# Edge stage of a graph convolution: second layer on the two halves of the array, first layer for four pairs at once

## What is computed

```python
h = silu(edge_scalars @ fc_w1 * (1.0 / sqrt(8))) * 1.679      # 8 -> 64
w = h @ fc_w2 * (1.0 / sqrt(64))                              # 64 -> 256
w_a, w_b, w_c, w_d = w[:, :64], w[:, 64:128], w[:, 128:192], w[:, 192:]
mid0 = w_a * xg0 * ea0
mid1 = w_b * einsum('euc,ec->eu', xg1, ea1) * INV_SQRT3
mid2 = (w_c * xg0)[:, :, None] * ea1[:, None, :]
mid3 = (w_d * ea0)[:, :, None] * xg1
agg = segment_sum(concat(mid0, mid1, mid2, mid3), edge_dst)   # 512 wide
```

## Time and profile before

| | |
|---|---|
| median of the runs | 4875.23 us |
| profiled execution, its time | 4926.35 us |
| its span | 4924.5 us |
| PE busy | 3152.5 us, 64% |
| DVE busy | 3139.1 us, 64% |
| POOL busy | 2963.7 us, 60% |
| ACT busy | 2579.5 us, 52% |
| mean granted clock of PE | 0.794 |
| instructions | 58380 |

### The profile page before, as it was taken

The page is one execution under the profiler, slowest core; times in us unless marked ns, Lnnn a source line. Parts: engine busy times, 40 slices in busy tenths (PEclk is TensorE's granted clock), DMA queues, the critical chain, the costliest instruction groups (busy, mean ns, idle before and its releaser), DMA issues. The chain is left out here.

```text
span 4924.5 us, 58380 instructions
## 1 busy us (share of the span) xinstructions
PE 3152.5 (64%) x11125; PEld 1913.5 (39%) x11125; DVE 3139.1 (64%) x8102; ACT 2579.5 (52%) x7839; POOL 2963.7 (60%) x3014
## 2 busy tenths in 40 slices
PE   4699989999999874545555565555354555555550
PEld 3344444444444563333433343333233333333340
DVE  7788888888888755454555554568354554555558
ACT  3588889888888522333333343345233343334347
POOL 2356656556556303667676676747667777776656
PEclk8899999999999987677767676678667777777675
DMA  5223233223223224444444444424444444444435
GB/s 165 90 83 86 84 86 88 84 85 87 83 84 90 75 82 125 121 118 129 122 122 127 116 126 128 116 72 138 117 115 128 128 116 129 127 115 128 120 91 160
DMA packets 274559, 540.42 MB, mean 110 GB/s; under 512 B 73156, under 2 KB 161983, under 8 KB 274240
## 3 DMA queue, kind: packets, MB, share of 16 engines
q0 software_dynamic: 134912, 376.36, 28.1%
q1 hardware_dynamic: 132308, 154.29, 10.0%
q10 hardware_dynamic: 7020, 6.40, 0.4%
HBM read 495.47 MB, written 41.31 MB: 109 GB/s over the span
## 5 line engine op out<-in xcount | busy, mean ns | idle before, releaser
L1174 POOL DMA_INDIRECT arena<-h_rows,idx x1856 | 1891.1, 1019 | 1070.9 <-issue 510.4
L1309 PE MATMUL ps<-arena,z 128*128 128x264 f32 x3712 | 1338.2, 514 | 455.3 <-DVE arena L1421 305.1
L768 POOL DMA_INDIRECT arena<-y_rows,idx x928 | 890.7, 960 | 730.1 <-ACT arena L799 361.5
L1233 ACT ACTIVATE z<-z 128x256 f32<-128x256 f32 x928 | 382.3, 412 | 1548.1 <-PE ps L1309 547.9
L1309 PEld LDWEIGHTS ps<-arena,z 128*128 128x128 f32 x3712 | 864.1, 251 | 694.1 <-DVE arena L1421 364.4
L1429 DVE TENSOR_TENSOR z<-ps,z 128x264 f32 x928 | 396.7, 427 | 1136.0 <-remote 378.7
L797 ACT ACTIVATE arena<-arena 128x128 f32<-128x128 f32 x2784 | 914.9, 399 | 12.7 <-issue 7.8
L842 PE MATMUL ps<-arena 128*128 128x512 f32 x1856 | 895.6, 606 | 14.5 <-issue 9.0
L1225 ACT ACTIVATE z<-iota,dst_x 128x128 f32<-128x128 f32 x1856 | 644.1, 394 | 26.4
L1421 DVE TENSOR_TENSOR arena<-arena,z 128x520 f32<-128x520 f32 x928 | 639.9, 690 | 2.1 <-ACT z L1214 1.3
L842 PEld LDWEIGHTS ps<-arena 128*128 128x128 f32 x1856 | 361.1, 196 | 485.4 <-issue 473.1
(11 more groups left out here) (229 smaller groups left out, 3070.1 us busy)
## 6 DMA issues: line engine op xcount, KB each, us to landing
z<-lo_rows SPq DMA_DIRECT2D x116, 512.0 KB
arena<-h_rows,idx POOLq DMA_INDIRECT x1856
arena<-y_rows,idx POOLq DMA_INDIRECT x928
z<-seg_rows SPq DMA_DIRECT2D x232, 64.0 KB
h_rows<-arena SPq DMA_DIRECT2D x98, 132.0 KB, 1.7
arena<-h_rows SPq DMA_DIRECT2D x98, 132.0 KB, 2.5
res_rows<-z SPq DMA_DIRECT2D x98, 128.0 KB, 1.9
arena<-res_rows SPq DMA_DIRECT2D x98, 128.0 KB, 2.1
```

The costliest lines, as they stand in the source:

```text
L768: pool.indirect_dma_start(out=ring[:, r, :], out_offset=None, in_=s.y_rows, in_offset=bass.IndirectOffsetOnAxis(ap=rows_of[:, u, n:n + 1], ...
L1174: pool.indirect_dma_start(out=ring[:, u * SCORED + n, :], out_offset=None, in_=h_rows, in_offset=bass.IndirectOffsetOnAxis(ap=s.idx[:, u, ...
L1233: nc.scalar.activation(sel[:, q % SELS, :, :].rearrange("p k n -> p (k n)"), away[:, q % 2, :, :].rearrange("p k n -> p (k n)"), ACT.Relu, ...
L1309: last = t.matmul(ps[:, bank[q % 4], 0:ROW], sel[:, q % SELS, k, :], ring[:, u * SCORED + 2 * q + k, :], start=(k == 0), stop=(k == 1))
```

## The change

In `conv_edges` alone:

- `second` is issued per quad: for each of its two pairs two matmuls, one on rows 0 to 63 and one on rows 64 to 127 of `h2` and `w2`, 256 columns each. `w2` is now fc_w2 twice, one under the other (128 x 256), without the zero blocks and their memset. The two slots of a pair go to two neighbouring banks (1 and 2, or 3 and 4 by quad), both pairs of a quad side by side in each. w_ok counts quads.
- `first` does four pairs (an octet) in one bank, 512 columns; with only one bank for it, it waits for the SiLU of the octet before. pre_ok and h_ok count octets.
- `silu` is one activation of 512 columns per octet, two `h2` buffers, the second in room freed by `w2` and next to it.
- PE's order: at pairs p with p % 4 = 3 `first` for octet (p + 9) // 4; at odd p `second` for the quad of pairs p + 3 and p + 4; then `collect`. ACT's order: the SiLU of octet p/4 + 1 ahead of `scaled`(p) for p % 4 = 0.
- `collect`, its three banks, and all of DVE's instructions but one memset stay; DVE's wait for w_ok counts quads, SP's for pre_ok octets.

```diff
-    h2 = s.arena[:, 8960:9472].rearrange("p (q a e) -> p q a e", q=2, a=2)
     tail = s.arena[:, 9472 + 4 * SLOT_COLS:2 * SCORED * ROW]
     ring = tail[:, 0:RING * FEAT].rearrange("p (r f) -> p r f", f=FEAT)
...
     ps = s.ps
-    w2 = tail[:, RING * FEAT + 4 * P:RING * FEAT + 8 * P]
-    pre = lambda quad: ps[:, quad % 2, 0:256]
-    layer2 = lambda pair: ps[:, 2 + pair % 3, :].rearrange("p (k f) -> p k f", k=2)
+    w2 = tail[:, RING * FEAT + 4 * P:RING * FEAT + 6 * P]
+    h2 = [s.arena[:, 8960:9472], tail[:, RING * FEAT + 6 * P:RING * FEAT + 10 * P]]
+    hidden = lambda pair: h2[pair // 4 % 2][:, pair % 4 * P:(pair % 4 + 1) * P]
+    pre = ps[:, 0, :]
+    halves = lambda quad: ps[:, 1 + quad % 2 * 2:3 + quad % 2 * 2, :]
+    layer2 = lambda pair: halves(pair // 2)[:, :, pair % 2 * FEAT:(pair % 2 + 1) * FEAT]
     collected = lambda pair: ps[:, 5 + pair % 3, :]
 
     with nc.Block() as block:
...
             for n in range(GROUP):
                 sp.dma_start(w8[8 * n:8 * n + 8, n // 2, n % 2 * 64:n % 2 * 64 + 64], a["fc_w1"]).then_inc(wt, 16)
...
+                sp.dma_start(w2[h * 64:(h + 1) * 64, :], a["fc_w2"]).then_inc(wt, 16)
             for pair in range(PAIRED):
 
...
-                    sp.wait_ge(pre_ok, (g - 1) * 4)
+                    sp.wait_ge(pre_ok, (g - 1) * 2)
                     sp.wait_ge(got8[u], g // 2 * 128)
...
-            def silu(quad):
-                act.wait_ge(pre_ok, quad + 1)
-                if quad >= 2:
-                    act.wait_ge(w_ok, 2 * (quad - 1))
-                nc.scalar.activation(h2[:, quad % 2, :, :].rearrange("p a e -> p (a e)"), pre(quad), ACT.Silu,
-                                     scale=1.0 / math.sqrt(8.0)).then_inc(h_ok, 1)
+            def silu(octet):
+                act.wait_ge(pre_ok, octet + 1)
+                if octet >= 2:
+                    act.wait_ge(w_ok, 2 * (octet - 1))
+                nc.scalar.activation(h2[octet % 2], pre, ACT.Silu, scale=1.0 / math.sqrt(8.0)).then_inc(h_ok, 1)
 
...
             silu(0)
-            silu(1)
             for pair in range(PAIRED):
-                quad = (pair - 3) // 2 + 2
-                if pair >= 3 and pair % 2 and quad < QUADS:
-                    silu(quad)
+                if pair % 4 == 0 and pair // 4 + 1 < OCTETS:
+                    silu(pair // 4 + 1)
                 if pair % 8 == 1 and pair // 8 + 3 < GROUPS:
                     stage(pair // 8 + 3)
                 scaled(pair)
...
-            def first(quad):
-                g, q = quad // 4, quad % 4
-                u = g % 2
-                if q == 0:
+            def first(octet):
+                g, u = octet // 2, octet // 2 % 2
+                if octet % 2 == 0:
                     pe.wait_ge(got8[u], (g // 2 + 1) * 128)
+                if octet >= 1:
+                    pe.wait_ge(h_ok, octet)
+                for n in range(4):
+                    last = nc.tensor.matmul(pre[:, n * P:(n + 1) * P], w8[:, octet % 2 * 4 + n, :], e8[:, u, :], start=True, stop=True)
+                last.then_inc(pre_ok, 1)
+
+            def second(quad):
+
+                pe.wait_ge(h_ok, quad // 2 + 1)
                 if quad >= 2:
-                    pe.wait_ge(h_ok, quad - 1)
-                for b in range(2):
-                    last = nc.tensor.matmul(pre(quad)[:, b * P:(b + 1) * P], w8[:, 2 * q + b, :], e8[:, u, :], start=True, stop=True)
-                last.then_inc(pre_ok, 1)
-
-            def second(pair):
-                quad = pair // 2
-                pe.wait_ge(h_ok, quad + 1)
-                if pair >= 3:
-                    pe.wait_ge(msg_ok, pair - 2)
-                nc.tensor.matmul(ps[:, 2 + pair % 3, :], h2[:, quad % 2, pair % 2, :], w2, start=True, stop=True).then_inc(w_ok, 1)
+                    pe.wait_ge(msg_ok, 2 * quad - 2)
+                for pair in (2 * quad, 2 * quad + 1):
+                    for k in range(2):
+                        rows = slice(k * 64, (k + 1) * 64)
+                        last = nc.tensor.matmul(layer2(pair)[:, k, :], hidden(pair)[rows, :], w2[rows, :], start=True, stop=True)
+                last.then_inc(w_ok, 1)
 
             def collect(pair):
                 pe.wait_ge(msg_ok, pair + 1)
@@ -842,24 +845,22 @@
                     last = nc.tensor.matmul(collected(pair), sel[:, pair % 4, k, :], msg[:, pair % 4, k, :], start=(k == 0), stop=(k == 1))
                 last.then_inc(agg_ok, 1)
 
-            for quad in range(4):
-                first(quad)
-                if quad < 2:
-                    second(2 * quad)
-                    if quad < 1:
-                        second(1)
+            first(0)
+            for quad in range(2):
+                second(quad)
+            first(1)
+            first(2)
             for pair in range(PAIRED):
-                if pair % 2 == 0 and pair // 2 + 4 < QUADS:
-                    first(pair // 2 + 4)
-                if pair + 3 < PAIRED:
-                    second(pair + 3)
+                if pair % 4 == 3 and (pair + 9) // 4 < OCTETS:
+                    first((pair + 9) // 4)
+                if pair % 2 and (pair + 3) // 2 < QUADS:
+                    second((pair + 3) // 2)
                 collect(pair)
 
...
             v.memset(s.w8[:, :], 0.0).then_inc(wz, 1)
-            v.memset(w2, 0.0).then_inc(wz, 1)
             v.memset(s.z[:, 0:BLOCKS * 512], 0.0).then_inc(zero_ok, 1)
...
                 v.tensor_tensor(vt, x[:, :, 448:512], x[:, :, 512:576], ALU.add).then_inc(v_ok, 1)
-                dve.wait_ge(w_ok, pair + 1)
+                dve.wait_ge(w_ok, pair // 2 + 1)
                 if pair >= 4:
                     dve.wait_ge(agg_ok, pair - 3)
                 three = lambda t: t.rearrange("p k (c f) -> p k c f", c=3)
```

4 lines of the change are left out of this document (2 added, 2 removed).

## The result

| | before | changed |
|---|---|---|
| median of the runs | 4876.36 us (4 runs) | 4950.77 us (4939.11 to 4959.67, 4 runs) |
| ratio | | 1.0126, 95% interval 1.0100 to 1.0153 |
| profiled execution | 4926.35 us | 4959.67 us |
| mean granted clock | 0.794 | 0.791 |

The forecast was 4774, in a range of 4690 to 4900: wrong in sign and outside the range. One sentence for everything that follows: the chips on which these kernels were measured differ, the kernel before taking 4459 to 4463 us on three and 4876 to 4918 on the others (these runs among them), so times are compared within one series only.

What follows compares the result with a forecast made beforehand. The prediction took PE, at 2.795 of 3.178 us a pair, to bound the edge stage. A lower floor (-30 us) and absorbed lateness (-71) gave -101, set against the median 4875.23: 4774 us, range 4690 to 4900.

Steps and rivals of the forecast that it cites:

- What bounds the kernel: Edge stage: PE is slowest at 2.795 us a pair of 3.178; the other 0.383 is stalls, 178 us over the stage.
- `second`: PE's second-layer matmuls: 0.86 us a pair becomes 0.54 by partial overlap of the halves, plus 0.16 for row switches.
- PE's sum: PE's time in the edge stage after the change: 2.64 us a pair, between 2.37 and 2.96 by the bounds.
- The floor: Slowest engine of the edge stage after the change: DVE with 2.73 us a pair instead of PE, ACT right behind.
- The gain of the floor: Edge stage: moving the bound from PE to DVE saves 0.065 us a pair over 464 pairs, 30 us.
- Lateness: Edge-stage stalls from late PE signals, taken as given: more slack absorbs four tenths of 178 us, a gain of 71 us.
- The bound that I had set aside: Edge-stage stalls: none of the 178 us is gained if lateness grows with the slack, as where PE's queue sets it.
- the size of the slack: Lateness consumers can bear: DVE 1.3 us before, 5 after, for its weights from PE.
- The SiLU's slack: ACT's room for late PE signals before its SiLU's wait for w_ok: 3.8 us before, 7.7 after.
- Rival 3: PE's `second`: halves don't overlap and switches are paid, 0.165 us a pair more, +77 us, 4952; chance 0.14.
- Rival 2: Edge stage: lateness follows PE's instruction count, 16 to 20 a pair, stalls 178 to 222 us, +14, 4889; chance 0.10.

Runs made afterwards that it cites:

- halves_apart: Changed kernel with the 64-row matmuls reordered, all of rows 0 to 63 first, then rows 64 to 127: 4428.28 us, ratio 0.9932 to the kernel before.
- second series: Runs on one chip with PE's signals on time: the unaltered changed kernel took 4429.71 us against 4458.93 for the kernel before, ratio 0.9933.
- octets_only: Kernel before with only `first` and SiLU per four pairs in one bank: ratio 0.9994 with signals on time; rerun as octets_only_2 with late signals, 4949.65 us, 1.0126.
- full_rows_w1: Changed kernel with `second` as one 128-row matmul per pair and w_ok given by each pair's matmul: 4922.26 us, ratio 1.0072 to before, signals late.
- before_more_pe: Kernel before with `first` in 64-column pieces, 20 PE weight loads and matmuls a pair instead of 16: 4561.81 us, 1.0231 on time; 0.997 in the late rerun.
- sp_light_before: Kernel before without SyncE's block-number load per pair: 4456.65 us, ratio 0.9992; the same edit on the changed kernel: 4425.99 us, 0.9923; signals on time.

## Why the prediction was wrong, by its own steps

- **What bounds the kernel.** Right: 2.795 us a pair of PE, measured 2.784 where nothing is late; 0.383 a pair of stalls, now 0.394.
- **`second`.** In full overlap, the lower bound; five steps of passes were taken, four ran. With its first switch it takes 0.53 a pair, and `collect` grew from 1.72 to 1.83, which I had not priced: together 0.64 against the 0.70 forecast for `second` and both switches. The Trainium skill (TensorE: Matmul & The Clock Gate, Part 3) has row groups running concurrently with starts about 4 ns apart; the trace agrees (6 to 7 ns). Beyond its four steps of 0.215 a quad costs 1.07 - 0.86 = 0.21 us, and its two `collect`s 3.66 - 3.44 = 0.22; no run isolates the two changes of rows in these 0.43. The Trainium skill (TensorEngine Tiling (Array Packing), Tiling Modes, Key Properties) has a change of mode drain TensorE, and the trace, with a cost at either side of `second`, doesn't speak against it.
- **PE's sum.** 2.64 forecast, 2.61 measured; that the passes overlap only as neighbours was a wrong step (halves_apart), and its price and the unpriced `collect` nearly cancel. **The floor** moves to DVE: 2.73 forecast, 2.722 measured. **The gain of the floor**: 30 us forecast, 29 measured in the second series. This half is right to a microsecond; as DVE sets the floor, the errors in PE's terms don't enter it.
- **Lateness, the step that failed.** The prediction took the lateness of PE's signals as given and asked how much each consumer can bear: four tenths of 178 us absorbed, 71 gained. Measured: 182 lost before and 272 after, 90 more instead of 71 less. The floor's -29 and these +90 make the 60 us by which the stage is longer. Two errors are in it. The first is the premise that the lateness is given: with holds of a given size the change does bear them better (27 us against 50), yet with the lateness that comes by itself its mean lag rises from 2.3 to 3.8 us. The bound that I had set aside, "nothing is taken if the lateness grows with the slack", was not even the end of it. The second is the size of the slack: a hold of 4.9 us cost the kernel before 0.65 us, not the 3.6 by which it exceeds 1.3, so 1.3 us was no measure of what it bears. The SiLU's slack was reckoned to go from 3.8 to 7.7 us, and 45 of 113 SiLUs still waited, 4.0 us each.
- **The other errors of that step.** I counted slack per signal and not what hangs on one. A SiLU for four pairs waits for the last of four matmuls and then frees, or stops, four pairs of work; `first`'s signal stood seven pairs ahead of its SiLU on ACT before and five now (four in octets_only). That this distance is the cause fits octets_only_2's 252 us against full_rows_w1's 167, and is argued, not shown.
- **Rival 3**, the other side, had the right sign for the wrong reason: 4952 forecast, 4951 measured, but the halves do overlap. A total that fits proves no mechanism.
- **Rival 2** had the right kind (more lateness, 4889) and the wrong cause: with the instructions alone the stage of before_more_pe loses less to lateness (117 us), not more.
- **Where the range failed.** Its upper end came from rivals 2 and 3 with the stalls as they were; no case had a floor that falls and lateness that grows by half.

Open stays why PE's signals are late on some chips, and why the grouping makes them later. In the trace of before 482 of SyncE's 3128 instructions between 210 and 1650 us take 0.7 us, where they otherwise take 0.02 to 0.44; two thirds of these (67%) fall in stretches in which a signal of PE is late, and 35% of the others. So they go with the late signals but are not confined to them, as the expectation of sp_light_before had it. On three chips neither is seen. That SyncE's own work has a part in it fits the stretches of loads above and is the rival left untested: no run with sp_light met a chip with late signals. Nor did the changed kernel itself run beside octets_only in one series on such a chip.

## What to carry to other kernels

When a stall comes from signals that arrive late, find out first whether it is there on every chip: here the same change is 0.7% faster on one and 1.3% slower on another. Don't count slack against a lateness taken from the trace of before, since lateness can grow with the program that is to bear it; keep signals early (full_rows_w1, with a bank more and `first` a pair earlier than octets_only_2, lost 0.7% instead of 1.3%), and look whether a signal that is grouped also starts another engine's work. Passes on different halves of the array overlapped in both orders tried, and PE's gain is kept only as far as PE was the bound.

## What was not expected of the hardware

- The 64-row fp32 matmuls of 256 columns overlap fully: eight passes in 1.07 us including a switch, in turn or one half after the other in the program (1.08).
- On three of the six chips of the experiments PE's signals were never more than 0.5 us late, in the six late profiles of the table up to 8 to 12 us, with 45 to 73% of them later than 0.5 us. The kernel before takes 415 to 457 us more where they are late; 182 lie in this stage in its one profile.
- Relaying every signal of PE through SyncE leaves a pair at 2.784 and 2.723 us; the 9 to 11 us that it costs lie mostly ahead of the first addition (215.9 and 214.1 us instead of 207). A hold of 4.9 us once in six pairs costs only 0.35 to 0.65 us each where signals are on time; one of 9.9 us, on a chip with late signals, made the stage 8.2 us longer.
